# A two-layer transformer block on one Trainium2 core: the prologue laid anew (order of the loads, of the first layer norm and of the first projections)

## What is computed

```
mod = silu(c) @ wmod                      # six rows of 512 per batch: shift, scale, gate, twice
h = layernorm(x) * (1 + ca) + sa
x = x + ga * attention(h)
h = layernorm(x) * (1 + cb) + sb
x = x + gb * ffn(h)
```

## Time and profile before

| | |
|---|---|
| runs | 2284.18, 2284.72, 2289.05 us (median 2284.72) |
| the profiled execution | 2288.48 us, span of its instructions 2286.7 us |
| PE busy | 2206.8 us, 97% of the span |
| DVE, ACT, POOL busy | 72%, 60%, 26% |

### The profile page before, as it was taken

The page is one execution under the profiler, slowest core; times in us unless marked ns, Lnnn a source line. Parts: engine busy times, 40 slices in busy tenths (PEclk is TensorE's granted clock), DMA queues, the critical chain, the costliest instruction groups (busy, mean ns, idle before and its releaser), DMA issues.

```text
span 2286.7 us, 40724 instructions
## 1 busy us (share of the span) xinstructions
PE 2206.8 (97%) x11084; PEld 1662.9 (73%) x11084; DVE 1642.3 (72%) x3030; ACT 1380.3 (60%) x2676; POOL 597.5 (26%) x437
## 2 busy tenths in 40 slices
PE   6999999999999989999999999999999999999978
PEld 4688888888887657777777777777777777776656
DVE  6577777777777657777777777777777777777856
ACT  2444444444444567777777777777777777776742
POOL 4456546556653440000000000000000000001432
PEclk9999999999999999999999999999999999999998
DMA  5101001001004142111111111111111111112341
GB/s 190 65 29 47 19 28 46 18 28 46 18 0 134 35 170 75 39 36 41 38 40 33 41 38 36 38 41 38 39 35 41 38 35 39 41 38 79 104 123 37
DMA packets 117152, 117.49 MB, mean 51 GB/s; under 512 B 28926, under 2 KB 71454, under 8 KB 117101
## 3 DMA queue, kind: packets, MB, share of 16 engines
q1 hardware_dynamic: 117100, 116.85, 16.9%
HBM read 95.30 MB, written 20.97 MB: 51 GB/s over the span
## 4 chain that ended last, share of the span: by engine, by line
PE 88%; DVE 5%; issue 2%; ACT 1%; DMA 1%; SPq 1%; POOL 1%; POOLq 0%; DVEq 0%; ACTq 0%
PE bank L2165 11%; PE bank L2152 10%; PE bank L2172 10%; PE bank L2183 10%; PE bank L1789 9%; PE bank L1791 8%; PE bank L1790 8%; PE bank L2083 5%; PE bank L2082 5%; PE bank L2081 5%; PE bank L1907 2%; DVE probs L1385 1%; DVE rope_b L1364 1%; DMA wm<-in_L_wmod 1%; DVE rope_a L1362 1%
## 5 line engine op out<-in xcount | busy, mean ns | idle before, releaser
L1597 DVE TENSOR_REDUCE mcol<-bank 128x1 fp32r<-128x512 f32 x1024 | 694.5, 689 | 346.9 <-PE bank L2152 341.4
L2165 PE MATMUL bank<-q,k 128*128 128x512 f32 x1024 | 418.7, 409 | 3.1 <-DMA k<-kc_d 1.9
L2152 PE MATMUL bank<-km,q 128*128 128x512 f32 x1024 | 405.9, 397 | 7.9 <-issue 4.7
L2172 PE MATMUL bank<-q,k 128*128 128x512 f32 x1024 | 405.7, 396 | 0.0
L747 POOL TENSOR_TENSOR wr_lo<-wst,wr_hi 128x512 fp32r<-128x512 f32 x64 | 81.6, 1276 | 1163.1 <-DVE wr_hi L1498 1163.1
L2152 PEld LDWEIGHTS bank<-km,q 128*128 128x128 f32 x1024 | 316.5, 309 | 59.1 <-issue 6.7
L1172 ACT ACTIVATE x<-bank 128x512 f32<-128x512 f32 x512 | 285.4, 601 | 87.0 <-PE bank L2172 82.6
L1172 ACT ACTIVATE pT<-bank 128x512 f32<-128x512 f32 x512 | 285.4, 601 | 85.2 <-PE bank L2172 81.8
L2165 PEld LDWEIGHTS bank<-q,k 128*128 128x128 f32 x1024 | 192.2, 188 | 129.6 <-issue 108.2
L2172 PEld LDWEIGHTS bank<-q,k 128*128 128x128 f32 x1024 | 192.2, 188 | 32.3
L2083 PE MATMUL bank<-hT_hi,wr_lo 128*128 128x512 f32 x512 | 202.9, 396 | 0.0
(11 more groups left out here) (297 smaller groups left out, 4146.8 us busy)
## 6 DMA issues: line engine op xcount, KB each, us to landing
wst<-in_L_attn_Wq_rope SPq DMA_DIRECT2D x64, 256.0 KB, 2.9
st_q<-in_L_attn_wq SPq DMA_DIRECT2D x8, 1024.0 KB, 7.0
st_wo<-in_L_attn_wo SPq DMA_DIRECT2D x8, 1024.0 KB, 5.1
km<-kc_d SPq DMA_DIRECT2D x256, 32.0 KB
q<-qc_d SPq DMA_DIRECT2D x256, 32.0 KB
k<-kc_d SPq DMA_DIRECT2D x256, 32.0 KB
o_d<-ost SPq DMA_DIRECT2D x512, 16.0 KB
wm<-in_L_wmod SPq DMA_DIRECT2D x6, 1024.0 KB, 10.1
```

The lines of the kernel that those rows point to most:

```text
L1597: dve.tensor_reduce(mcol[:, k % 2, i % 4, i // 4:i // 4 + 1], bank[4 + i % 2][:], AX.X, ALU.max, negate=True)\
L2152: pe.matmul(bank[4 + i % 2][:], q2[:, k % 4, h, i % 4:S:4], km[:, b, h], start=True, stop=True).then_inc(max_mm, 1)
L2165: pe.matmul(bank[s % 4][:], k1[:, k % 2, t], q1[:, k % 4, h], start=True, stop=False)
L2172: pe.matmul(bank[s % 4][:], k2[:, k % 2, h, t], q2[:, k % 4, h], start=False, stop=True).then_inc(scores1, 1)
```

## The change

Six things, all in the prologue:

1. SP's order: the identity and batch 0's tiles of x first, then two `wmod` chunks, K and V weights, constants, Q weights, and only then batch 1's tiles and the other chunks. `load_kv` is split into `load_k_v` and `load_q`.
2. `xn0` and `full0` lie where `wo_hi`, `wo_lo`, `oT_hi`, `oT_lo` and `gate_a0` are written later, so that the rotary tiles and `bq0` are free from the start.
3. K and V of batch 0 are projected in pieces of three matmuls (`first_part`), one per tile of 128 features, as soon as that tile is split.
4. Batch 1's norm (all engines) and the chunks 2 to 5 of `mod` stand between the projections of batch 0.
5. `clamp_gates(0)`, `broadcast_gate(0, 0)` and `gates(0, 0)` stand ahead of `kv_head(0)`, not inside it.
6. PSUM banks of the first norm and of the first columns are others.

No arithmetic is added or taken away. Cut to its core:

```diff
+        with ExitStack() as before_wo:
+            xn0 = sbuf_in(before_wo)("xn0", [P, NT, D])
...
+        with ExitStack() as before_oT:
+            full0 = sbuf_in(before_oT)("full0", [P, 4, S])
...
-            xn0 = sbp("xn0", [P, NT, D])
-            full0 = sbp("full0", [P, 4, S])
+            sbp("q_pad", [P, 12, S])
...
+            if ph == 0:
+                return bank[(0, 1, 4, 5)[j % KT]]
...
-            return bank[((0, 5), (7, 5))[l][half]][:, 0:16]
+            return bank[((2, 5), (7, 5))[l][half]][:, 0:16]
...
-            for t in range(NT):
-                sp.dma_start(x[:, t], x_in[:, t]).then_inc(x_moved[t // TB], 16)
+            sp.dma_start(ident[:], a["identity"]).then_inc(ident_loaded, 16)
+
+            def load_x(b):
+                for t in range(TB * b, TB * b + TB):
+                    sp.dma_start(x[:, t], x_in[:, t]).then_inc(x_moved[b], 16)
 
...
-            def load_kv(n):
+            def load_k_v(n):
                 if exists(n, HKV):
-                    hold(w_split, 6 * n)
                     sp.dma_start(st_kv[:, 0], wk_v[:, :, bass.ts(n, HD)]).then_inc(kv_loaded, 16)
                     sp.dma_start(st_kv[:, 1], wv_v[:, :, bass.ts(n, HD)]).then_inc(kv_loaded, 16)
+
+            def load_q(n):
+                if exists(n, HKV):
                     sp.dma_start(st_q[:], wq_v[:, :, bass.ts(n, GQ * HD)]).then_inc(q_loaded, 16)
...
-            sp.dma_start(ident[:], a["identity"]).then_inc(ident_loaded, 16)
-            sp.dma_start(sel[:], a["batch_rows"].rearrange("p (b m) -> p b m", b=B)).then_inc(ident_loaded, 16)
+            load_x(0)
             sp.dma_start(rowsum[:], a["four_identities"]).then_inc(ident_loaded, 16)
             load_wmod(0)
             load_wmod(1)
-            load_kv(0)
-            load_wmod(2)
+            load_k_v(0)
             sp.dma_start(rope_cos[:], a["rope_cos"]).then_inc(rope_loaded, 16)
             sp.dma_start(rope_sin[:], a["rope_sin"]).then_inc(rope_loaded, 16)
+            sp.dma_start(sel[:], a["batch_rows"].rearrange("p (b m) -> p b m", b=B)).then_inc(rope_loaded, 16)
             sp.dma_start(window[:], a["window_mask"]).then_inc(rope_loaded, 16)
+            load_q(0)
+            load_x(1)
+            load_wmod(2)
             load_wmod(3)
             load_wmod(4)
+            load_wmod(5)
             load_wo(0)
-            load_wmod(5)
             with sp.Fori(1, HKV) as n:
-                load_kv(n)
+                hold(w_split, 6 * n)
+                load_k_v(n)
...
-            split_weights(0, (0, 1))
-            norm(0, 0)
+            def norm_low(b, j):
+
+                pool.wait_ge(ln_hi, j + 1)
+                pool.tensor_tensor(hT_lo[:, j % KT, b * S:(b + 1) * S], full0[:, j % 4], hT_hi[:, j % KT, b * S:(b + 1) * S].bitcast(F32),
+                                   ALU.subtract).then_inc(ln_lo_odd, 1)
+
+            split_weights(0, (0,))
+            split_weights(0, (1,))
+            norm_low(0, 1)
             split_weights(0, (2,))
-            norm(0, 1)
-            split_weights(0, (3, 4, 5))
-            wait_norm(pool, 0, 1)
-            for name in ROPE_NO:
-                rope(0, name, 0)
-            rope(1, "K", 1)
+            norm_low(0, 3)
+            rope_add(0, "K", 0)
+            split_weights(0, (3,))
+            rope_low(0, "K", 0)
+            split_weights(0, (4,))
+            split_weights(0, (5,))
+            rope_add(0, "Q0", 0)
+            rope_add(0, "Q1", 0)
+            rope_low(0, "Q0", 0)
+            rope_low(0, "Q1", 0)
+            norm_low(1, 5)
+            norm_low(1, 7)
+            rope_add(0, "Q2", 0)
+            rope_add(0, "Q3", 0)
+            rope_low(0, "Q2", 0)
+            rope_low(0, "Q3", 0)
+            rope_add(1, "K", 1)
+            rope_low(1, "K", 1)
...
-            for b in range(B):
-                norm_std(0, b)
-            mod_rows(0, (0, 1))
-            for b in range(B):
-                norm(0, b)
-
...
-                    if isinstance(n, int) and n == 0 and b == 0:
-                        gates(0, 0, gate_a0)
...
+            norm_std(0, 0)
+            mod_rows(0, (0,))
+            mod_rows(0, (1,))
+            norm(0, 0, (0,))
+            norm(0, 0, (1,))
+            norm(0, 0, (2,))
+            norm(0, 0, (3,))
+            norm_std(0, 1)
+            norm(0, 1, (4,))
+            norm(0, 1, (5,))
+            norm(0, 1, (6,))
+            norm(0, 1, (7,))
+            mod_rows(0, (2,))
             rope_high(0, "K", 0)
+            v_high(0, 0)
+            mod_rows(0, (3,))
             rope_high(0, "Q0", 0)
             rope_high(0, "Q1", 0)
-            v_high(0, 0)
+            mod_rows(0, (4,))
+            mod_rows(0, (5,))
             rope_high(0, "Q2", 0)
             rope_high(0, "Q3", 0)
-            mod_rows(0, (2, 3, 4, 5))
+            exps(0, 0)
             rope_high(1, "K", 1)
-            exps(0, 0)
+            gates(0, 0, gate_a0)
             kv_head(0, False)
...
+            norm_rows(0, 0)
+            split_weights((0,))
+            split_weights((1,))
+            mod_cols(0, 0)
+            norm_split(0, 0, (0,))
+            norm_split(0, 0, (1,))
+            norm_split(0, 0, (2,))
+            split_weights((2,))
+            norm_split(0, 0, (3,))
             norm_stats(0, 1)
-            norm_rows(0, 0)
+            split_weights((3,))
+            split_weights((4,))
+            split_weights((5,))
             norm_rows(0, 1)
-            mod_cols(0, 0)
-            split_weights((0, 1))
-            norm_split(0, 0)
-            split_weights((2, 3))
-            norm_split(0, 1)
-            split_weights((4, 5))
-            dve.wait_ge(rope_loaded, 48)
-            for name in TURN:
-                evacuate(0, name, 0)
+            evacuate(0, "K", 0)
+            norm_split(0, 1, (4,))
+            evacuate(0, "V", 0)
+            norm_split(0, 1, (5,))
+            evacuate(0, "Q0", 0)
+            evacuate(0, "Q1", 0)
+            evacuate(0, "Vt", 0)
+            norm_split(0, 1, (6,))
+            norm_split(0, 1, (7,))
+            evacuate(0, "Q2", 0)
+            evacuate(0, "Q3", 0)
+            mod_cols(0, 1)
+            clamp_gates(0)
             evacuate(1, "K", 1)
-            mod_cols(0, 1)
             mask(0, 0)
+            normalise(0, 0)
             evacuate(1, "V", 1)
-            normalise(0, 0)
-            clamp_gates(0)
...
+                    if c == 2:
+                        pe.wait_ge(col_ready, 1)
...
+                if l == 0 and c == 2:
+                    pe.wait_ge(ln_full, NT)
...
-            pe.wait_ge(ident_loaded, 48)
-            pe.wait_ge(silu_step, 5)
-            mod(0, 0)
-            norm(0, 0)
-            mod(0, 1)
-            mod_use(0, 0)
-            mod_use(0, 1)
-            pe.wait_ge(col_ready, 1)
-            norm(0, 1)
+            def norm_tile(b, t):
+
+                if b == 1 and t == 0:
+                    pe.wait_ge(ln_full, KT)
+                pe.wait_ge(ln_norm, TB * b + t + 1)
+                for k in range(KT):
+                    e = pe.transpose(norm_bank(0, k)[:, t * P:(t + 1) * P], xn0[:, TB * b + t, k * P:(k + 1) * P], ident[:])
+                e.then_inc(ln_trans, 1)
+
+            def first_part(name, k):
+
+                m = W_TILE[name]
+                ps = bank[6 + TURN[name]]
+                if k == 0:
+                    pe.wait_ge(w_split, m + 1)
+                pe.wait_ge(ln_lo_odd if k % 2 else ln_lo, k // 2 + 1)
+                pe.matmul(ps[:], w_hi[:, m, k], hT_hi[:, k, 0:S], start=(k == 0), stop=False)
+                pe.matmul(ps[:], w_hi[:, m, k], hT_lo[:, k, 0:S], start=False, stop=False)
+                e = pe.matmul(ps[:], w_lo[:, m, k], hT_hi[:, k, 0:S], start=False, stop=(k == KT - 1))
+                if k == KT - 1:
+                    e.then_inc(proj_done, 1)
 
...
+                if isinstance(half, int) and half == 1 and name == "K":
+                    wait_norm(pe, 0, 1)
...
-                        broadcast_gate(0, 0)
...
-            wait_norm(pe, 0, 0)
-            for name in TURN:
-                project(0, name, 0, 0)
-            wait_norm(pe, 0, 1)
-            project(1, "K", 1, 0)
+            pe.wait_ge(ident_loaded, 32)
+            pe.wait_ge(silu_step, 5)
+            mod(0, 0)
+            norm_tile(0, 0)
+            mod_use(0, 0)
+            mod(0, 1)
+            norm_tile(0, 1)
+            norm_tile(0, 2)
+            mod_use(0, 1)
+            norm_tile(0, 3)
+            first_part("V", 0)
+            first_part("K", 0)
+            first_part("V", 1)
+            first_part("K", 1)
+            first_part("K", 2)
             mod(0, 2)
+            first_part("V", 2)
+            first_part("K", 3)
+            norm_tile(1, 0)
+            norm_tile(1, 1)
+            norm_tile(1, 2)
+            norm_tile(1, 3)
             mod(0, 3)
+            first_part("V", 3)
+            project(0, "Q0", 0, 0)
```

(23 more changed lines are left out.)

## The result

| | kernel before | changed kernel |
|---|---|---|
| median, 5 runs each on one chip | 2285.51 us (2284.18 to 2294.93) | 2268.47 us (2264.67 to 2269.49) |
| the same once more, 11 and 6 runs | 2285.78 us (2278.61 to 2292.23) | 2268.14 us (2263.88 to 2272.76) |
| profiled execution, its span | 2288.48 us, 2286.7 us | 2268.89 us, 2267.0 us |

The ratio is 0.9913, 95% interval 0.9891 to 0.9935, and the second time 0.9923 (0.9903 to 0.9943). The kernel is 17 us faster; 18.7 had been forecast, with 2266.0 us.

A forecast was written before the change was run, and what follows sets the result against it. PE was taken to bound the kernel (88% of the span). Scores at 56.7 plus 1.3, 2.8 and 2.0 put `kv_head(0)` at 62.8; 81.5 - 62.8 saves 18.7 us, giving 2266.0 us, range 2262.0 to 2274.0.

The forecast's parts named there:

- the mark: Start of half 1's Q1 projection, 87.05 us in the kernel before, taken as the start of steady work.
- Part 1: Prologue loads: less data ahead of the first wmod chunk, so PE starts at 11.8 and `full` at 20.5, 3.1 us sooner.
- Part 2: K and V pieces on batch 0: hidden behind DVE, with K evacuated from 31.6 to 33.7 us.
- Part 3: From K's evacuation to the scores: POOL sets the pace, 19.7 us of operations plus 3.3 of waits, scores at 56.7.
- rival 2: Prologue: everything runs warm, with transposes and `mod(0, 3)` at full clock; saving up to 22, time 2262.7 us; chance 0.11.
- Part 4: Scores to the steady loop: scores 1.3, V 2.8 and the gate's product 2.0 us, so `kv_head(0)` starts at 62.8.
- T: The new start of `kv_head(0)`, forecast at 62.8 us; the kernel would end 81.5 - T earlier.
- The sum: Whole kernel: 81.5 - 62.8 = 18.7 us saved, the median going from 2284.72 to 2266.0 us; chance 0.64.
- Rival 1: Prologue projections and scores: PE stays at 1.2 GHz; saving 11.4 to 15.4, time 2269.3 to 2273.3 us; chance 0.18.
- Rival 4: Between K's pieces: the late third chunk blocks PE, slower from 47 us on, 2290 at 52; chance 0.03.
- rival 3: Later in the kernel: a date that doesn't move, say `st_wo`, gives the gain back; saving 0 to 4; chance 0.04.
- The clock rule: Batch 1's transposes: taken to bring up PE's clock, so Q0 runs at full clock, against the Trainium skill's rule.

The follow-up runs named there:

- e2: The changed kernel with the old order of loads up to the window mask: 2272.03 us, ratio 0.9912 to the kernel before.
- e1: The kernel before with only SP's new order of loads: 2302.53 us, ratio 1.0045 to the kernel before.
- e5: The changed kernel with unread identity products, 8 ahead of the first chunk and 6 ahead of the first projection piece: 2265.63 us, ratio 0.9898.
- e3: The changed kernel with K and V of batch 0 projected whole, not in pieces: 2273.15 us, ratio 0.9926 to the kernel before.
- e7: The changed kernel with DVE evacuating Q2 before it splits batch 1's last two tiles: 2271.45 us, ratio 0.994 to the kernel before.
- e4: The changed kernel with the first gate's broadcast and copy back inside kv_head(0): 2273.48 us, one run.
- e11: The changed kernel itself, run and profiled again without any edit: 2268.14 us, ratio 0.9923 to the kernel before.
- e7b: The changed kernel with DVE evacuating Q2 before batch 1's last two tiles, and POOL's list reordered to match: 2275.34 us, ratio 0.9934.
- e9: The changed kernel with transposes of the identity (16 and 12) as fillers in two idle stretches of PE: 2269.5 us, ratio 0.9904.

## Why the prediction was right, and where it was wrong

The time (2266.0 forecast, 2268.5 and 2268.1 measured) lies in the range, but two of its steps failed. At the mark the saving was 2.4 us more than forecast, and from the mark to the medians 4.1 us of it are missing. That the two errors have opposite signs and leave the sum 1.7 us off is luck.

- **Part 1, loads: right.** 11.8 said, 10.63 found. The loads' own share is as forecast: e2, with the old loads, starts PE at 13.82, 3.2 us later. The other 1.1 us lie between that 13.82 and the 14.88 of the kernel before, which has the same loads up to there, and the first landing moves by that much between executions (last section). ACT's `full` 20.5 said, 19.90 found. e1 shows that the loads need DVE's new order. The third chunk was hidden, as said: 26.94 without a wait. With PE 2 us sooner it is not (e5, 1.57 us).
- **Part 2, "the pieces as such are hidden behind DVE": wrong.** The first piece came at 22.02 (22.4 said), K's evacuation at 30.71 (31.6 said), on DVE behind `xn` as forecast. But e3 loses 5.7 us. The step looked only at when K's result is evacuated. It missed that PE has no slack behind: what the 24 products of K and V do not do while the norm runs, they do later, and all of PE's list moves with them, with Q1's end and so DVE's and POOL's part of the chain. The lower clock was counted for 13 matmuls to 28.0; it was over at 24.7 after 6.
- **Part 3, "POOL sets the pace", 56.7: wrong step.** The scores began at 54.40. POOL started 0.8 us sooner, at 32.88. Its 15 operations took 21.0 us, not 19.7; the longest (1.75 us for one, 3.17 for two) ran while DVE wrote `hT_hi` and `hT_lo` of batch 1. The term that failed is the wait: 0.8 us in place of the 3.3 worked out. 2.0 of those 3.3 came from the lower clock given to batch 1's transposes and `mod(0, 3)`, by rival 2's own figures; they took 1.94 and 1.06 us, not 3.63 and 1.91. Nor is it POOL that sets the pace: in the chain above it has only the last three operations, behind 11.0 us of DVE, which the forecast did not add up for this stage. PE's own list ended at 53.88, 0.52 us before the scores. e7 shows how little slack there is: it evacuates Q2 sooner, and POOL then waits 1.69 us for batch 1's tiles, which are later. The timeline of POOL, the longest of these rows and one that waits:

```profile
34.37 1.75 POOL L666 TENSOR_TENSOR w_lo<-st_q,w_hi 128x512 fp32r<-128x512 f32 x1
...
42.72 3.17 POOL L684 TENSOR_TENSOR bq_lo<-rope_a,bq_hi 128x512 fp32r<-128x512 f32 x2
...
50.38 1.28 POOL L676 TENSOR_TENSOR rope_a<-rope_a,rope_b 128x512 f32<-128x512 f32 x1 [0.59 <-DVE rope_b L1407]
```

- **Part 4: right.** Scores 1.39 us (1.3 said), the gate's 1.98 in its place, 5.32 from T to the mark (5.54 said), and behind it PE has one wait of 0.5 us more than before in the next 70 us. T is 60.62 (62.8 said). e4 confirms the gate's share: 3.4 us, where 3.15 were counted.
- **The sum.** 21.1 us at the mark against 18.7 forecast, as rival 2 (all of it warm, up to 22) had it, and by its mechanism: the transposes and `mod(0, 3)` ran at the full clock, which had risen by 24.7. The median's saving is 17, in the forecast's own bracket and not near rival 2's time. The step that failed there is the silent one that the rest of the kernel moves as one block: it does so only within its scatter of 5 us. The ratio's interval, 14.9 to 24.9 us, holds the mark's 21.1. The kernel before was profiled once, in an execution 3.0 us above its median, and its front may vary as that of the changed kernel does (3.4 us, e11). Whether the last 4 us are scatter alone, the runs do not settle.
- **Rival 1** did not happen in the changed kernel. e7b shows its mechanism, with 3.2 us of cost, at the scores, one of the places it named. **Rival 4** did not happen. Of **rival 3** nothing is seen: PE waits for no DMA from 22.02 to 400 us.
- **The clock rule.** Before, the clock rose at the end of 3.6 us of nothing but transposes, and now stayed at 1.00 over sixteen of them (1.94 us at 29.58, against 3.63 for sixteen at the lower clock). The Trainium skill, "TensorE: Matmul & The Clock Gate", part on the PE-mode transpose, says that the full clock does not engage for transposes. By it these would have taken 3.63 us, and the trace of the changed kernel disagrees. What the forecast read from the earlier trace rows was half of the story, though: the same transposes had begun with a fall of the clock (full rate up to 23.5, 0.50 from 24 on). Letting Q0 run at full clock was right, and the reason given for it is not secured (e9).

## What to carry to other kernels

Date a prologue by the first instruction of the steady stretch, and count PE's time up to there in two heaps, standing still and lower clock; here they were 13.8 and 7.3 of 21.1 us, and in one execution a wait of 1.74 us cost another 3.2 in clock. Before an engine is declared the bound, add up the lists of all engines, PE's at full clock, and follow the chain back from the product in question: where two lists end within half a microsecond, work that PE does earlier is not hidden, and exchanging two steps on DVE or POOL gained nothing. Profile the changed kernel twice before small variants are compared with it: a gain of 2 us at the mark was no more than what another execution of the same program gave.

## What was not expected of the hardware

- The same program came to the full rate of PE at 14.5 us in one execution and at about 17.5 in another, with landings equal to 0.03 us. In e7b, with the same list, it had not come to it by its first piece at 25.30.
- The column of the granted clock does not show this: it reads 1.00 over the time in which eight products took 1.93 us that take 1.06 at the full rate. In the first microseconds the durations tell the clock. PE alone, of the changed kernel, while such products run:

```profile
15.00:16.00 1.00, 1.00 (x9) 1.00 1.06 365
```

- The first landing moves by itself: with the same list of loads the first chunk started PE at 10.47 to 10.97 us in six executions (the changed kernel, e1, e3, e4, e7, e11), and at 12.36 in e7b, which is 1.7 of that run's later mark.
